# A transformer layer with attention and a routed expert layer: the shared expert of groups 4 to 7 run behind the expert blocks, and the second residual formed by ScalarE and TensorE

## The reference

```python
def _performer_attn(x, wq, wk, wv, wo, omega):      # 16 heads of 8, 32 features each
    pq, pk = _phi(q * scale, omega), _phi(k * scale, omega)
    kv, z  = einsum('bhsm,bhsk->bhmk', pk, v), sum(pk, axis=2)
    out = (pq @ kv) / (pq @ z)[..., None]
    return out @ wo

h  = _performer_attn(x, ...)
x  = layernorm(x + h, ln1_g, ln1_b)
h2 = gelu(x @ w1 + b1) @ w2 + b2                    # 128 -> 512 -> 128
x  = layernorm(x + h2, ln2_g, ln2_b)
```

```python
shared   = silu(x_flat @ shared_w1.T) @ shared_w2   # for every row
gates    = softmax of the two largest of x_flat @ gate_w.T
selected = sum over the two chosen experts of gate * (silu(x @ w1[e].T) @ w2[e].T)
out      = x + layernorm(shared + selected)
```

## Time and profile before

| | us |
|---|---|
| median of 3 runs | 598.88 |
| lowest and highest of the runs | 595.96, 599.67 |
| the profiled execution, its time | 594.31 |
| its span in the trace | 592.6 |
| pipeline, from the first transpose of k = 5 to the last scatter's end | 176 to 382 |
| first and last matmuls of the expert blocks | 404 to 547 |

### The profile page before, as it was taken

The page is one execution under the profiler, slowest core; times in us unless marked ns, Lnnn a source line. Parts: engine busy times, 40 slices in busy tenths (PEclk is TensorE's granted clock), DMA queues, the critical chain, the costliest instruction groups (busy, mean ns, idle before and its releaser), DMA issues.

```text
span 592.6 us, 10592 instructions
## 1 busy us (share of the span) xinstructions
PE 460.4 (78%) x3392; PEld 355.3 (60%) x3392; DVE 316.1 (53%) x1298; ACT 261.4 (44%) x540; POOL 245.2 (41%) x368
## 2 busy tenths in 40 slices
PE   3899999999979888867727657598999999997000
PEld 2577766676655555656514435377989888987000
DVE  6887785786573578799865312301322222222394
ACT  2655544445434566644734213234445444443053
POOL 7300000110001134237887775500655555656592
PEclk9999999999998999987978777788999999999555
DMA  8920010000000000000001111330222222221622
GB/s 271 359 71 19 6 32 1 2 2 1 2 0 1 0 2 1 2 1 19 28 33 43 47 55 37 102 83 1 69 82 74 73 74 73 77 65 38 244 108 88
DMA packets 17843, 33.88 MB, mean 57 GB/s; under 512 B 4128, under 2 KB 10528, under 8 KB 17536
## 3 DMA queue, kind: packets, MB, share of 16 engines
q1 hardware_dynamic: 12096, 21.68, 11.4%
q0 software_dynamic: 4544, 9.45, 4.8%
q10 hardware_dynamic: 1152, 2.10, 0.9%
HBM read 19.65 MB, written 13.56 MB: 56 GB/s over the span
## 4 chain that ended last, share of the span: by engine, by line
PE 58%; DVE 14%; POOL 8%; issue 7%; ACT 5%; another core or an unknown queue 4%; DMA 2%; SPq 0%; POOLq 0%; DVEq 0%; ACTq 0%
PE pQKV L869 6%; PE pF L587 5%; POOL xs L489 4%; PE pPK L585 3%; PE pPK L587 3%; PE pPK L586 3%; PE pKV L662 3%; PE pF L585 3%; PE pQKV L831 3%; PE pPQ L869 3%; PE pF L586 3%; PE pQKV L785 2%; PE pPK L778 2%; PE pF L691 2%
## 5 line engine op out<-in xcount | busy, mean ns | idle before, releaser
L437 POOL TENSOR_TENSOR ve<-mv,eps 128x4 f32<-128x4 f32 x40 | 9.5, 238 | 209.3 <-DVE mv L1081 208.9
L556 POOL DMA_INDIRECT ys<-MID,PQT x78 | 76.0, 974 | 24.8 <-issue 24.8
L489 POOL DMA_INDIRECT xs<-PL,SLOT x64 | 64.1, 1001 | 20.0 <-issue 20.0
L1395 DVE TENSOR_SCALAR MID<-pQKV,PQT 128x128 f32<-128x128 f32 x40 | 12.2, 347 | 83.6 <-remote 66.4
L441 POOL TENSOR_TENSOR rs<-ve,halves 128x4 f32<-128x4 f32 x40 | 42.5, 1061 | 3.1
L869 PE MATMUL pQKV<-E,HT 128*128 x320 | 39.1, 275 | 1.2 <-ACT HT L1037 1.2
L585 PE MATMUL pPK<-XFH,E1H 128*128 128x512 f16 x32 | 15.3, 478 | 31.6 <-ACT MID L1015 15.3
L869 PEld LDWEIGHTS pQKV<-E,HT 128*128 128x128 f32 x320 | 37.3, 192 | 1.6 <-issue 1.4
L869 PE MATMUL pPQ<-E,HT 128*128 x304 | 37.3, 276 | 0.6 <-DVE MID L1395 0.6
L430 POOL TENSOR_TENSOR held<-halves 128x1 f32<-128x1 f32 x47 | 9.2, 195 | 67.7 <-DVE MID L1395 57.9
L869 PEld LDWEIGHTS pPQ<-E,HT 128*128 128x128 f32 x304 | 35.5, 192 | 1.2 <-issue 0.9
(11 more groups left out here) (258 smaller groups left out, 1302.3 us busy)
## 6 DMA issues: line engine op xcount, KB each, us to landing
PQT<-xs SPq DMA_DIRECT2D x39, 132.0 KB
PQT<-in_ew1T SPq DMA_DIRECT2D x1, 2304.0 KB, 9.7
E<-in_ew2T SPq DMA_DIRECT2D x1, 2304.0 KB, 9.9
X<-in_x SPq DMA_DIRECT2D x8, 256.0 KB, 6.8
HT<-in_ew1T SPq DMA_DIRECT2D x8, 256.0 KB, 4.3
PQT<-ys SPq DMA_DIRECT2D x4, 512.0 KB
ys<-MID,PQT POOLq DMA_INDIRECT x78
xs<-PQT SPq DMA_DIRECT2D x8, 132.0 KB
```

The costliest lines, as they stand in the source:

```text
L489: eng.indirect_dma_start(xs, bass.IndirectOffsetOnAxis(SLOT[:, g, t, a:a + 1], 0), PL[:, g, t, a, :], None).then_inc(s_scat[g], 16)
L556: eng.indirect_dma_start(ys, bass.IndirectOffsetOnAxis(XS[q][:, t, ID_AT:ID_AT + 1].bitcast(U32), 0), Y[q][:, t, :], None).then_inc(s_ysc[ ...
```

## The change

Two edits:

1. The shared expert of groups 4 to 7 leaves the pipeline. TensorE and ScalarE do it after their last expert block, in the functions `late_up`, `late_down`, `late_silu` and `late_out`. ScalarE has all of it ahead of its first `norm_sum`. VectorE waits for `SUM[n]` of each group in the tail; TensorE's start of the blocks waits for the four shared results of the pipeline in place of eight.
2. `x2`, the row form of the residual, is no longer made by VectorE. ScalarE reads `pT` a second time and writes `X2T`, with `b2` in the bias; TensorE turns it back with the identity into `pQKV`, ahead of the down matmuls, which accumulate on it. VectorE's L1255, L1257 and L1275 go. Statistics and norm read the bank `pQKV`, so the down matmul of the next group waits for the norm of this one (`s_no[2]`) where it waited for `s_r2`.

```diff
@@ TensorE, pipeline
                 if k == 5:
-                    wait(pe, s_x1t, n)
+                    wait(pe, s_x2t, n)
                 if k == 8:
-                    wait(pe, s_r2, n)
+                    wait(pe, s_no[2], n)
+                    pe.wait_ge(s_x2t, n + 1)
                     pe.wait_ge(s_ge, (n + 1) * FC)
                     for t in range(T):
+                        nc.tensor.matmul(pQKV[:, t * P:(t + 1) * P], X2T[:, t * P:(t + 1) * P], ident[:],
+                                         start=True, stop=False)
                         for c in range(FC):
                             m = nc.tensor.matmul(pQKV[:, t * P:(t + 1) * P], HT[:, c, t * P:(t + 1) * P],
-                                                 w2_s[:, c, :], start=(c == 0), stop=(c == FC - 1))
+                                                 w2_s[:, c, :], start=False, stop=(c == FC - 1))
-                if k == SHARED:
+                if k == SHARED and n < GB:
-                if k == SHARED + 3:
+                if k == SHARED + 3 and n < GB:
@@ TensorE, before and behind the blocks
-            pe.wait_ge(s_sh, NG)
+            pe.wait_ge(s_sh, GB)
+            def late_up(m):
+                for c in range(EC):
+                    pe.wait_ge(*((s_ss1, (m - 1) * EC + c + 1) if m > GB else (s_si, 2 * NBLK)))
+                    three(banks[c][:], [v[:, 0, c * P:(c + 1) * P] for v in (E1H, E1L)],
+                          [XFH[:, m % GB], XFL[:, m % GB]]).then_inc(s_su, 1)
+            def late_down(m):
+                pe.wait_ge(*((s_sh, m - 1) if m >= GB + 2 else (s_bl, NBLK)))
+                pe.wait_ge(s_ss1, (m + 1) * EC)
+                for t in range(T):
+                    for c in range(EC):
+                        s = nc.tensor.matmul(turned[m % 2][:, t * P:(t + 1) * P], HSL[m % 2][:, c, t * P:(t + 1) * P],
+                                             E2[:, 0, c, :], start=(c == 0), stop=(c == EC - 1))
+                s.then_inc(s_sd, 1)
+            late_up(GB)
+            for m in range(GB, NG):
+                if m + 1 < NG:
+                    late_up(m + 1)
+                late_down(m)
@@ ScalarE
-                    norm_act(2, n, R2)
+                    norm_act(2, n, pQKV)
                     A(X1T, pT[:], ACT.Identity, scale=cols_s[:, 0:1], bias=cols_s[:, 1:2]).then_inc(s_x1t, 1)
+                    wait(act, s_dn, n)
+                    A(X2T, pT[:], ACT.Identity, scale=cols_s[:, 0:1], bias=b12[:]).then_inc(s_x2t, 1)
-                if k == SHARED:
+                if k == SHARED and n < GB:
-                if k == SHARED + 4:
+                if k == SHARED + 4 and n < GB:
+            def late_silu(m):
+                if m >= GB + 2:
+                    act.wait_ge(s_sd, m - 1)
+                for c in range(EC):
+                    act.wait_ge(s_su, m * EC + c + 1)
+                    A(HSL[m % 2][:, c, :], banks[c][:], ACT.Silu, scale=wunscale[:]).then_inc(s_ss1, 1)
+            def late_out(m):
+                act.wait_ge(s_sd, m + 1)
+                A(SUM[m], (pT, pKV)[m % 2][:], ACT.Copy).then_inc(s_sh, 1)
+            late_silu(GB)
+            for m in range(GB, NG):
+                if m + 1 < NG:
+                    late_silu(m + 1)
+                late_out(m)
@@ VectorE
-                if k == 6:
-                    dve.wait_ge(s_no[1], n + 1)
-                    x2, n1 = (u.rearrange("p (t d) -> p t d", t=T) for u in (XN[:, n], N1))
-                    v.tensor_tensor(x2, n1, rows_s[:, 0, :]...to_broadcast([P, T, D]), ALU.mult).then_inc(s_n1g, 1)
-                    v.tensor_tensor(x2, x2, b12[:]...to_broadcast([P, T, D]), ALU.add).then_inc(s_x2, 1)
                 if k == 9:
-                    wait(dve, s_no[2], n)
-                    dve.wait_ge(s_x2, n + 1)
                     dve.wait_ge(s_dn, n + 1)
-                    v.tensor_tensor(R2, pQKV[:], XN[:, n], ALU.add).then_inc(s_r2, 1)
-                    hold(s_r2, n + 1)
-                    stats(2, n, R2)
+                    stats(2, n, pQKV)
...
+                dve.wait_ge(s_sh, max(GB, n + 1))
                 v.tensor_tensor(acc, acc, y[:, :, 0], ALU.add).then_inc(s_acc, 1)
...
-            dve.wait_ge(s_sh, NG)
```

More of the change, by code:

```diff
@@ L103, in build @@
         wo_s = sb("wo_s", [P, P])
-        cols_s = sb("cols_s", [P, 2 + FC])
-        rows_s = sb("rows_s", [P, 5, P])
-        b12 = sb("b12", [P, P])
+        cols_s = sb("cols_s", [P, 3 + FC])
+        rows_s = sb("rows_s", [P, 2, P])
+        b12 = sb("b12", [P, 1])
         w1_s = sb("w1_s", [P, FF])
@@ L148, in build @@
         MID = sb("MID", [P, 5, GW])
-        N1, R2 = (MID[:, i, :] for i in range(1, 3))
+        N1, X2T = (MID[:, i, :] for i in range(1, 3))
         NY = [MID[:, 3, :], MID[:, 4, :]]
@@ L228, in build @@
         YC = list(parts(pq, *[2 * GW] * 4)) + list(parts(mid, *[2 * GW] * 2)) + list(
-            parts(E2[:].rearrange("p e c d -> p (e c d)"), *[2 * GW] * 2))
+            parts(E2[:].rearrange("p e c d -> p (e c d)")[:, EC * D:], *[2 * GW] * 2))
         W1S = HT
+        HSL = [XN[:, GB:NG], XN[:, 0:GB]]
         HS = [[HT[:, c, :] for c in range(EC)], [MID[:, 0, :]] + list(parts(pq, *[GW] * (EC - 1)))]
@@ L261, in build @@
             sem("recip_spread"), sem("recip_turned"), sem("attn"), sem("wo_done"), sem("res1"))
-        s_nT, s_x1t, s_up, s_ge, s_dn, s_r2 = (sem(n) for n in (
-            "n1_turned", "x1t", "up_done", "gelu_done", "down_done", "res2"))
+        s_nT, s_x1t, s_up, s_ge, s_dn = (sem(n) for n in (
+            "n1_turned", "x1t", "up_done", "gelu_done", "down_done"))
         s_n2g, s_y2, s_x1 = sem("n2_times_g"), sem("y_ready"), sem("x1_ready")
@@ L344, in _ @@
             sp.dma_start(EW1.rearrange("p (e h) -> p e h", e=E + 1), ew1T).then_inc(s_ew1, 16)
-            sp.dma_start(rows_s[:].rearrange("p v d -> p (v d)"), rows.to_broadcast([P, 5 * P])).then_inc(s_w, 16)
+            sp.dma_start(rows_s[:].rearrange("p v d -> p (v d)"), rows.to_broadcast([P, 2 * P])).then_inc(s_w, 16)
             sp.dma_start(cols_s[:], cols).then_inc(s_w, 16)
@@ L535, in _ @@
             pool.wait_ge(s_w, 16 * NLOADS)
-            eng.tensor_tensor(b12[:], rows_s[:, 1, :], rows_s[:, 2, :], ALU.add).then_inc(s_const, 1)
+            eng.tensor_tensor(b12[:], cols_s[:, 1:2], cols_s[:, 2 + FC:3 + FC], ALU.add).then_inc(s_const, 1)
             pool.wait_ge(s_const, NCONST + 1)
@@ L1248, in stage @@
                     wait(dve, s_nT, n)
-                    wait(dve, s_n1g, n)
                     norm(1, n, tiles(N1), XN[:, n])
-                if k == 6:
-                    dve.wait_ge(s_no[1], n + 1)
-                    x2, n1 = (u.rearrange("p (t d) -> p t d", t=T) for u in (XN[:, n], N1))
-                    v.tensor_tensor(x2, n1, rows_s[:, 0, :].unsqueeze(1).to_broadcast([P, T, D]), ALU.mult).then_inc(s_n1g, 1)
-                    dve.wait_ge(s_n1g, n + 1)
-                    v.tensor_tensor(x2, x2, b12[:].unsqueeze(1).to_broadcast([P, T, D]), ALU.add).then_inc(s_x2, 1)
                 if k == 14:
@@ L1280, in stage @@
                     y = NY[n % 2].rearrange("p (t d) -> p t d", t=T)
-                    v.tensor_tensor(y, y, rows_s[:, 3, :].unsqueeze(1).to_broadcast([P, T, D]), ALU.mult).then_inc(s_n2g, 1)
+                    v.tensor_tensor(y, y, rows_s[:, 0, :].unsqueeze(1).to_broadcast([P, T, D]), ALU.mult).then_inc(s_n2g, 1)
                     dve.wait_ge(s_n2g, n + 1)
-                    v.tensor_tensor(y, y, rows_s[:, 4, :].unsqueeze(1).to_broadcast([P, T, D]), ALU.add).then_inc(s_y2, 1)
+                    v.tensor_tensor(y, y, rows_s[:, 1, :].unsqueeze(1).to_broadcast([P, T, D]), ALU.add).then_inc(s_y2, 1)
                     hold(s_y2, n + 1, at=3)
@@ L1455 @@
         "cols": np.concatenate([f("L0_attn_ln1_g")[:, None], f("L0_attn_ln1_b")[:, None],
-                                f("L0_attn_b1").reshape(FC, P).T], axis=1),
-        "rows": np.concatenate([f(f"L0_attn_{n}") for n in ("ln1_g", "ln1_b", "b2", "ln2_g", "ln2_b")])[None, :],
+                                f("L0_attn_b1").reshape(FC, P).T, f("L0_attn_b2")[:, None]], axis=1),
+        "rows": np.concatenate([f(f"L0_attn_{n}") for n in ("ln2_g", "ln2_b")])[None, :],
         "w1": f("L0_attn_w1"),
```

4 lines of the change are left out of this document (2 added, 2 removed).

## The result

The changed kernel takes 622.88 us (median of 4 runs, 621.03 to 626.22), the kernel before beside it 597.92 us (595.96 to 599.67). The ratio is 1.0425, with a 95% interval from 1.0367 to 1.0482. The profiled execution took 621.03 us, its span is 619.3 us; before it was 594.31 and 592.6. So in the trace there are 26.7 us to find.

What follows compares the result with a forecast made beforehand. Bound: waits through VectorE in the rounds, then GpSimd's scatters, TensorE in the blocks, VectorE in the tail. +18.8 (first scatter) + 5 (clock) - 14.7 (blocks' start) + 6.4 (tail) = +15.5 on 598.88: 614.4 us; own range 605 to 623, stated 603 to 624.

Steps and rivals of the forecast that it cites:

- four rounds, loop: Pipeline rounds of groups 4 to 7: down waits for ScalarE's norm, holding up L705 and VectorE's division; +20.8 us together.
- four rounds, clock: TensorE's idle waits ahead of down lower its clock: three stretches of 1.7 us, +5 us, range 0 to 9.
- fifth round: Round without L705, ahead of the first scatter: down ends before VectorE wants it, VectorE's saving comes through; -2.0 us.
- start of the blocks: First scatter to blocks: -14.2 us for starting at the first load, -2 for SLOT, +1.5 for low clock; -14.7.
- tail: Behind the blocks: the late shared expert delays ScalarE's first norm_sum and VectorE's first residual add; +6.4 us, 5 to 8.
- a late start of the round: First of the four rounds: the down part ahead of it has the identity too, so it starts 0.9 us late.
- the -2 for the SLOT of the last group: Among the scatters: GpSimd's 2.84 us wait for group 7's SLOT shrinks; gain between 0 and 3.8 us, taken as 2.
- The signs: Profile after: rounds about 20 us, waits of 4 to 6 ahead of down, first scatter 293 to 299, blocks 110 to 117 later.
- VectorE's saving decides: Rival: down doesn't hold up L705, four rounds save 2.0 us each; sum -16.4, 582.5 us; chance 0.08.
- The clock stays low: Rival: half clock through down and up in four rounds and longer at the blocks' start; +28, 627 us; chance 0.08.
- Part of the loop is slack: Rival: each round grows by only 2 to 4 us and the clock stays; 597 to 605 us; chance 0.10.

Runs made afterwards that it cites:

- dummies in the wait: Changed kernel with 3, 5, 5 and 5 matmuls whose result nobody reads, ahead of the down matmuls' wait in groups 1 to 4; 604.36 us, ratio 1.0175.
- part 1 alone: Kernel before with only the shared expert of groups 4 to 7 moved behind the blocks, the residual as before; 592.11 us, ratio 0.9887.
- part 2 alone: Kernel before with only the residual moved to ScalarE and TensorE, the shared expert as before; 630.06 us, ratio 1.0528.
- splitting: Part 1 alone, with four of the eight filler writes issued by ScalarE and four by SP; 582.13 us, ratio 0.9789.
- the copied kernel: Changed kernel, but VectorE copies the bank to XN, statistics and norm read the copy, and down waits for the copy; 599.66 us, ratio 1.0010.
- the interleaved list: Part 1 alone, with ScalarE's norms of groups 0 and 1 put ahead of its last copies of the shared result; 583.44 us, ratio 0.9823.
- the kernel with the bank copied, the reciprocal first and both mends: The copied kernel, with TensorE turning the reciprocal ahead of down, the interleaved list, and filler writes split between SP and ScalarE; 588.08 us, ratio 0.9853.

## Why the prediction came out as it did

The forecast was +15.5 us, 614.4, and the medians say +25.0, 622.88: inside the range of 603 to 624, with the mechanism that was named, and 8.5 us above the likeliest value. That it lies inside by 1 us is in part luck. The two profiled executions are 26.7 us apart, which is more than the +24 at which the forecast's own range ended; the medians are 25.0 apart, and the forecast started 1.0 us above the median of the runs beside the change. Point by point, from the traces:

| term | forecast | measured | by |
|---|---|---|---|
| ahead of the rounds | 0 | +1.9 | the trace after |
| four rounds, loop | +20.8 | +19.3 | dummies in the wait (80.6 - 61.3) |
| four rounds, clock | +5 | +8.7 | after against the dummies (89.3 - 80.6) |
| fifth round | -2.0 | -0.5 | the trace after |
| start of the blocks | -14.7 | -8.8 | -9.7, and 0.9 in the blocks |
| tail | +6.4 | +6.1 | the trace after |
| sum | +15.5 | +26.7 | |

*The loop* was right. With the clock held up, the second to fourth rounds are 20.0, 20.8 and 22.4 us, where 20.15, 20.85 and 22.5 were worked out; the first is 17.5 for 18.6. There the prediction added 0.9 us for a late start of the round; but from the first transposition of the pipeline to the first L699 it is 18.8 us after and 18.7 before, so this term isn't there. The brackets ahead of down are 2.8 to 5.2 us, released by ScalarE's norm.

*The clock* was mis-sized, by 3.7 us. I counted three stretches of 1.7 us. There were four, each 1.8 to 2.4 us: the bracket of 2.77 us in the first round was followed by 0.50 as well, and half clock lasted through more than half of down, which is longer by the identity. The prediction's "0 to 9" held it. The Trainium skill (TensorE: Matmul & The Clock Gate, section HAM oscillation) states that repeated waits bring the array back to half rate each time. The traces agree in all four rounds: 0.50 is granted behind each wait, and 1.00 in the kernel whose dummies fill the waits.

*The fifth round* brought 0.5 us, not 2.0. The prediction took down as done 1.3 us before VectorE wants it. It took 7.2 us there too (291.63 to 298.85, 0.50 granted from 292 to 296 us), and VectorE waits for it:

```profile
299.05 0.89 DVE L1121 BATCH_NORM_STATS2 st<-pQKV 128x6 f32<-128x128 f32 x4 [0.81 <-PE pQKV L789]
```

Another 0.44 us it waits for the output matmul at 288.43, which the removed L1255 and L1257 used to hide. These two waits are 1.25 us of the missing 1.5.

*The start of the blocks* is the term that was furthest off, 5.9 us, as the prediction feared of it. The load lands 2.2 us after its issue, not 3, so this gives -15.1 for -14.2. The filler writes start 99.4 us after the first scatter (99.2 before), so nothing is left of the -2 for the SLOT of the last group. And SP's filler writes, which the prediction took as unchanged, take 5.3 us more from the first of them to the load. The blocks themselves became 0.9 us longer, where 1.5 was put down for the cold clock.

For part 1 alone the -2 was borne out: there the fillers start 95.7 us after the first scatter, 3.5 us earlier than before. Part 2 took it back, by GpSimd's wait of 3.86 us for VectorE's statistics at 350.59: part 2 alone has this wait too, and its fillers start 103.1 us after the first scatter. The prediction held that in later rounds the scatters cover the new wait, and worked that out for the first of them only.

*Why the fillers are slower* stays open. Shown is that the long ones occur only beside the scatters (1.07 us each without), that two queues get them done sooner (splitting gives 5.9 us back), and that TensorE's idleness is not the cause. It isn't simply that the shared expert is gone either: the two kernels with it in the pipeline took 11.6 and 11.9 us, and those without it, with all eight writes on SP beside the scatters, 15.8 to 18.2, but the one with dummies in the rounds took 11.1. It starts its fillers 15.1 us ahead of the last scatter's start, the others 8 to 9, but the copied kernel, with 12.7, took 18.2. No run tells what decides.

*The tail* came out as worked out. Its cause, the late shared expert ahead of the first norm in ScalarE's list, is shown by the interleaved list for 5.0 of the 8.1 us by which part 1 alone has the longer tail; the other 3.1 aren't traced.

*The signs.* The brackets ahead of down, their releaser, the missing VectorE rows and the first norm 25.2 us after the end of the last block's matmuls (592.60, "some 26") are as the prediction said. The first scatter at 303.0 us lies outside its 293 to 299, and the blocks' start 120.9 us after it outside its 110 to 117: the clock, the fifth round and the fillers, as above.

*The rivals.* "VectorE's saving decides" was rightly held unlikely, but its price was wrong too. It gave VectorE 2.0 us a round as soon as down didn't wait. The copied kernel takes the wait away and puts one of the three steps back, so 1.4 us a round should come through, and its rounds are 0.8 to 0.9 us longer instead: the two other steps stood beside TensorE's down and L705, and the identity lengthened just these. "The clock stays low" (+28 in all) came near the measured number, yet for another reason: half clock did not last through up. "Part of the loop is slack" is excluded: the rounds grew by 5.9 to 7.9 us, not 2 to 4. That statistics on the bank cost nothing more, which the prediction took from VectorE's adds, the trace after confirms (next section).

## What to carry to other kernels

Before adding a wait to an in-order queue, list what stands behind it and who needs that: here a down part that could well wait held up a short transposition (eight matmuls, 1.06 us) for which VectorE waited, and moving it ahead gave back 15 us of 28. As the copied kernel shows, an engine's removed work counts only where the other engine's path to the same meeting point is shorter; the time by which it is the later one there (0.12 us here, of 1.4 removed) is the most that can come through. And work moved to an idle stretch behind the last block still stands in some engine's list ahead of the epilogue: interleave it there.

## What the runs showed of the hardware that was not expected

Groups by line and shape, changed kernel (busy us, mean ns of one, then idle before):

```profile
L1121 DVE BATCH_NORM_STATS2 st<-pQKV 128x6 f32<-128x128 f32 x32 | 7.0, 281 | 18.9 <-PE pQKV L789 13.3 <-remote 5.6
L1121 DVE BATCH_NORM_STATS2 st<-XN 128x6 f32<-128x128 f32 x32 | 6.9, 280 | 0.3
...
L995 ACT ACTIVATE MID<-MID,nm,rs 128x128 f32<-128x128 f32 x32 | 13.1, 479 | 0.0
L995 ACT ACTIVATE MID<-pQKV,nm,rs 128x128 f32<-128x128 f32 x32 | 11.8, 446 | 0.0
```

A bn_stats of 128x128 takes VectorE 281 ns from the bank and 280 ns from SBUF. A norm of the same size takes ScalarE 446 ns from the bank and 479 from SBUF, so there the bank is the faster source, by 33 ns.

The other is the price of a direct DMA from SP beside GpSimd's indirect ones: 1.07 us for each write of 132 KB alone, and on average 1.4 to 2.3 us where all eight go out from SP beside the scatters, with up to 7.0 us from one to the next.

The length of a wait alone didn't tell here whether the clock would fall. After 2.77 us of an idle TensorE in the changed kernel 0.50 was granted. In the kernel with the bank copied, the reciprocal first and both mends, TensorE waits 1.38 us ahead of L706 in each of the first three rounds. In the second round L706 then takes 1.16 us, with 1.00 granted from 218 to 222 us; in the third it takes 2.03 us, with 0.50 granted from 232 to 235.
